# Attention adds moved to GpSimd by blocks, extra tiles at places 4 to 17, two tables made among the shared units, no closing GpSimd drain

## The reference, cut to what matters

```python
xn = layernorm(x)
# attention: each of 8 heads x 4 points picks one channel of the batch's first token
off = (xn @ W_off + b_off).reshape(B, N, 8, 4, 2)
w   = softmax((xn @ W_attn + b_attn).reshape(B, N, 8, 4), axis=-1)
idx = clip(wrap(int(off[..., 0])), 0, 127)
s   = sum(xn[:, 0, idx] * w)                     # one number per token
attn = broadcast(s, 128) @ W_out + b_out         # = s * colsum(W_out) + b_out
# feed-forward: 2 shared experts for all tokens, the best 2 of 8 routed ones per token
ffn(x, w1, w2, w3) = silu(x @ w1.T) * (x @ w3.T) @ w2.T
out = x + attn + sum(shared ffn) + sum(cw[e] * ffn_e(xn) for the 2 chosen e)
```

## Time and profile before

| | us |
|---|---|
| median of 3 runs | 418.75 (418.43 to 419.17) |
| span of the profiled execution | 416.8 |
| PE busy | 366.9 (88%) |
| DVE busy | 331.8 (80%) |
| ACT busy | 190.5 (46%) |
| POOL busy | 189.7 (46%) |

### The profile page before, as it was taken

One profiled execution on the slowest core, in us unless ns is written; L12 is line 12 of the kernel. 1 busy time (PEld: TensorE's weight loads), 2 busy tenths in 40 slices (PEclk: granted clock), 3 DMA queues, 4 the chain that ended last, 5 costly groups with the idle time before them and its releaser, 6 DMA issues.

```text
span 416.8 us, 12515 instructions
## 1 busy us (share of the span) xinstructions
PE 366.9 (88%) x4333; PEld 316.9 (76%) x4333; DVE 331.8 (80%) x929; ACT 190.5 (46%) x446; POOL 189.7 (46%) x152
## 2 busy tenths in 40 slices
PE   0157797789999999999999999999999999999990
PEld 0155564467677777777779999999999999999990
DVE  5988989987967699999996998886666666666760
ACT  2778728395322466666666344422222222222220
POOL 0434500404777776343200000001888888888863
PEclk9988999999999999999999999999999999999997
DMA  8944620000117199988873345554565956654332
GB/s 298 296 97 104 126 77 0 2 0 16 48 56 167 57 187 179 182 166 165 168 110 60 75 132 159 131 133 118 67 63 67 79 62 66 65 65 39 35 34 19
DMA packets 98871, 41.36 MB, mean 99 GB/s; under 512 B 73600, under 2 KB 92416, under 8 KB 98816
## 3 DMA queue, kind: packets, MB, share of 16 engines
q1 hardware_dynamic: 87120, 31.82, 36.7%
q0 software_dynamic: 11264, 8.69, 16.0%
q10 hardware_dynamic: 432, 0.11, 0.1%
HBM read 10.94 MB, written 12.88 MB: 57 GB/s over the span
## 4 chain that ended last, share of the span: by engine, by line
PE 74%; DVE 13%; ACT 6%; DMA 2%; issue 1%; POOL 1%; POOLq 0%; DVEq 0%; ACTq 0%
PE pY L832 18%; PE pY L655 11%; PE pAB L806 8%; PE pAB L804 8%; PE pAB L805 8%; PE pAB L643 5%; PE pAB L645 5%; PE pAB L644 5%; PE pV L667 4%; ACT units L870 3%; DVE hbuf L1189 2%; ACT wsp L941 2%; PE pV L621 2%; DVE hot L1095 1%; DMA xT<-hot 1%
## 5 line engine op out<-in xcount | busy, mean ns | idle before, releaser
L1065 POOL DMA_INDIRECT out_dram<-xT,rows x64 | 99.1, 1549 | 104.6 <-DMA out_dram<-base 83.3
L1011 ACT ACTIVATE units<-pAB 128x512 f32<-128x512 f32 x78 | 46.5, 596 | 119.6 <-PE pAB L806 119.6
L1053 POOL DMA_INDIRECT sorted_rows<-rows,slot x64 | 67.2, 1050 | 59.0 <-issue 32.3
L805 PE MATMUL pAB<-rows,wsp 128*128 128x128 f16 x512 | 89.0, 219 | 0.0
L806 PE MATMUL pAB<-rows,wsp 128*128 128x128 f16 x512 | 89.0, 219 | 0.0
L804 PE MATMUL pAB<-rows,wsp 128*128 128x128 f16 x512 | 89.0, 219 | 0.0
L832 PE MATMUL pY<-wsp,hbuf 128*128 (+1 forms) x620 | 86.4, 282 | 0.3 <-issue 0.3
L1476 DVE SCALAR_TENSOR_TENSOR hbuf<-pAB,units 128x512 f32<-128x512 f32 x78 | 53.6, 687 | 31.7 <-PE pAB L806 29.3
L832 PEld LDWEIGHTS pY<-wsp,hbuf 128*128 128x128 f32 x620 | 75.6, 192 | 0.8 <-issue 0.5
L655 PE MATMUL pY<-wsp,hbuf 128*128 128x128 f32 x512 | 70.2, 280 | 0.0
L655 PEld LDWEIGHTS pY<-wsp,hbuf 128*128 128x128 f32 x512 | 64.3, 192 | 4.1
(11 more groups left out here) (164 smaller groups left out, 586.1 us busy)
## 6 DMA issues: line engine op xcount, KB each, us to landing
base<-in_x SPq DMA_DIRECT2D x8, 512.0 KB, 7.5
out_dram<-base SPq DMA_DIRECT2D x16, 256.0 KB, 2.4
wraw<-in_wall SPq DMA_DIRECT2D x10, 256.0 KB, 2.8
rows<-hot SPq DMA_DIRECT2D x8, 256.0 KB, 2.7
proj<-sorted_rows SPq DMA_DIRECT2D x27, 68.5 KB, 1.9
wsp<-in_wall SPq DMA_DIRECT2D x10, 128.0 KB
sorted_rows<-rows,slot POOLq DMA_INDIRECT x64, 2.4
out_dram<-xT,rows POOLq DMA_INDIRECT x64, 3.4
```

What stands on the lines that cost most here:

```text
L805: pe.matmul(o, hi, x(1), start=False, stop=False)
L1053: pool.indirect_dma_start(sorted_rows, bass.IndirectOffsetOnAxis(ap=slot[:, t:t + 1].bitcast(U32), axis=0), rows[:, t, :], None, bounds_ch ...
L1065: pool.indirect_dma_start(out_rows, bass.IndirectOffsetOnAxis(ap=meta[:, t, DEST - CW:DEST - CW + 1].bitcast(U32), axis=0), yt[:, t], None ...
```

## The change

- **Extras at places 4 to 17.** `EXTRA_FROM` goes from 8 to 4. The list of jobs is otherwise the same.
- **Attention by blocks on GpSimd.** `r_attention` leaves VectorE's job loop (64 instructions of 128 elements). GpSimd gets `add_attention`: for each of the 16 blocks a product of `csum` and `attn_all` to a buffer of two (512 elements) and an addition to `base` (512 elements), the addition one block behind. It stands between the sorting scatters and the sends, and starts when `attn_saved` and `y_read` are complete.
- **Writes of blocks.** `WRITE_AT` now puts block i behind the loads of the turn eight after the one that ends with place i or later.
- **Tables.** `spread` is made before unit 22, straight behind the routing, in another buffer (`small`). TensorE's product and ScalarE's copy of it come with unit 25, and the copy lies in fp16 in a new buffer `sides16`, whose space `wp_raw` and `ident32` use before. `extra_table` follows before unit 24.
- **No GpSimd drain.** The `Block` is opened with `no_gpsimd_drain=True`.

```diff
-SPREAD_UNIT = UNITS - 4
+SPREAD_UNIT, SIDES_UNIT = 22, 25
...
-EXTRA_FROM = 8
+EXTRA_FROM = 4
...
-WRITE_AT = [min(n for n in range(AHEAD, STEPS) if FIRST_OF_TURN[n - AHEAD + 1] >= TPB * (i + 1) // ADDS + 5) for i in range(NB)]
+WRITE_AT = [min(n for n in range(AHEAD, STEPS) if LAST_OF_TURN[n - AHEAD] >= i) for i in range(NB)]
...
-        block = ctx.enter_context(nc.Block())
+        block = ctx.enter_context(nc.Block(no_gpsimd_drain=True))
...
+                if n == SIDES_UNIT:
+
+                    pe.wait_ge(table_ready, 1)
+                    pe.wait_ge(spread_ready, 1)
+                    for b in range(2):
+                        mm = pe.matmul(pV[:, b, :], c["ones"][:], spread.rearrange("p t m -> p (t m)")[:, b * BLK:(b + 1) * BLK],
+                                       start=True, stop=True)
+                    mm.then_inc(sides_done, 1)
...
-                if q == 1:
-                    spread_sides()
...
+                if n == SIDES_UNIT:
+                    act.wait_ge(sides_done, 1)
+                    nc.scalar.copy(sides16[:], pV[:].rearrange("p b c -> p (b c)")).then_inc(sides_ready, 1)
...
+            def add_attention():
+
+                for i in range(NB + 1):
+                    if i < NB:
+                        if i == 0:
+                            pool.wait_ge(attn_saved, APAIRS)
+                            pool.wait_ge(y_read, NB)
+                        if i >= 2:
+                            pool.wait_ge(attn_added, i - 1)
+                        nc.gpsimd.tensor_tensor(attn_part[:, i % 2], csum[:].unsqueeze(1).broadcast_to([P, TPB, P]),
+                                                attn_all[:, TPB * i:TPB * (i + 1)].unsqueeze(2).broadcast_to([P, TPB, P]),
+                                                ALU.mult).then_inc(attn_scaled, 1)
+                    if i:
+                        pool.wait_ge(attn_scaled, i)
+                        row = base[:, TPB * (i - 1):TPB * i, :]
+                        nc.gpsimd.tensor_tensor(row, row, attn_part[:, (i - 1) % 2], ALU.add).then_inc(attn_added, 1)
+
+            add_attention()
             pool.wait_ge(out_done, 16 * NB)
...
+            while unit[0] < SPREAD_UNIT:
+                shared_unit()
+            spread_out()
+            while unit[0] < ROUND * ATT - 8:
+                shared_unit()
+            extra_table()
...
-                if q == 1:
-                    extra_table()
...
-            def r_attention(g, r):
-                q = UNROLL * g + r
-                for tile in range(ADDS * q, min(ADDS * (q + 1), NT)):
-                    ins = add_attention(tile)
-                    if tile % TPB == TPB - 1:
-                        ins.then_inc(attn_added, 1)
```

More of the change, by code:

```diff
@@ L340, in layer_kernel @@
         yt = xT[:].rearrange("p i j s c -> p (i j s c)").bitcast(F32).rearrange("p (t c) -> p t c", c=P)
-        spread = hot_row[:, 0:TILES * 2 * E].rearrange("p (t m) -> p t m", m=2 * E)
-        sides = early[:, 512:1536].rearrange("p (t k e) -> p t k e", k=2, e=E)
+        spread = small[:].rearrange("p r c -> p (r c)").bitcast(F16).rearrange("p (t m) -> p t m", m=2 * E)
+        sides = sides16[:].rearrange("p (t k e) -> p t k e", k=2, e=E)
+        attn_part = aw_row[:, 0:2 * BLK].rearrange("p (r j c) -> p r j c", r=2, j=TPB)
         share_w = early[:, 1536:1664].rearrange("p (t k) -> p t k", k=2)
@@ L435, in layer_kernel @@
         attn_saved = sem("attn_saved")
+        attn_scaled = sem("attn_scaled")
         attn_added = sem("attn_added")
@@ L620, in routing_products @@
                     for a in range(NPAIR):
-                        mm = pe.matmul(pV[:, 1, 256:256 + NT], ident32[:], place[:, a, :], start=(a == 0), stop=(a == NPAIR - 1))
+                        mm = pe.matmul(pV[:, 1, 256:256 + NT], ident32, place[:, a, :], start=(a == 0), stop=(a == NPAIR - 1))
                     mm.then_inc(place_done, 1)
@@ L755, in _ @@
             straight(UNITS - ROUND, UNITS, both + [(0, first_addresses, UNITS - ROUND, UNITS)])
[L756 to L763, removed]
             def r_turn(g, r):
@@ L844, in _ @@
         def _(act):
-            for dst, src in [(wp_raw[:], wproj), (c["ident"][:], const["ident"]), (bp[:], bproj)]:
+            for dst, src in [(wp_raw, wproj), (c["ident"][:], const["ident"]), (bp[:], bproj)]:
                 act.dma_start(dst, src).then_inc(first_in, 16)
@@ L926, in exponentials @@
                 if n == ROWS_UNIT:
-                    nc.scalar.copy(ident32[:], c["ident"][:]).then_inc(ident_ready, 1)
+                    nc.scalar.copy(ident32, c["ident"][:]).then_inc(ident_ready, 1)
                     for r in range(4):
@@ L1412, in routed_low @@
                     split_low(g - (ATT - 1), u // 4)
[L1415 to L1422, removed]
             def extra_table():
@@ L1434, in extra_table, with spread_out @@
                 v.scalar_tensor_tensor(active[:], f(0), 0.0, f(1), ALU.is_gt, ALU.mult).then_inc(extras_ready, 1)
[L1436 to L1443, removed]
+            def spread_out():
+                dve.wait_ge(table_done, 1)
+                v.tensor_tensor(spread, c["ident"][:, 0:TILES].unsqueeze(2).broadcast_to([P, TILES, 2 * E]),
+                                tab_f[:, 2:2 + 2 * E].unsqueeze(1).broadcast_to([P, TILES, 2 * E]),
+                                ALU.mult).then_inc(spread_ready, 1)
+            while unit[0] < SPREAD_UNIT:
[4 more added lines that the diff above has]
+            extra_table()
+            assert unit[0] == ROUND * ATT - 8
+            for n in range(8):
+                shared_unit()
+                one_hot(ATT - 1 + (n + 4) // ROUND, (n + 4) % ROUND)
+                if n >= 6:
+                    weighted_high(ATT - 1, n)
             start, end = ROUND * ATT, UNITS
@@ L1450, in _ @@
             rounds(dve, ATT + 1, UNITS // ROUND - 1, both)
-            straight(UNITS - ROUND, UNITS + 4, both + [(0, spread_out, UNITS - ROUND, UNITS)])
+            straight(UNITS - ROUND, UNITS + 4, both)
             extra_tile = {}
@@ L1546, in y_second @@
                                            ).then_inc(d_y, 1)
[L1548 to L1561 removed]
             pipeline(dve, NJOB, UNROLL, NJOB // UNROLL, [(4, side_sums), (4, y_first), (4, y_second), (2, r_hf), (3, side_products),
[L1563 removed]
+                                                         (4, load_tiles), (2, extra_shares)])
 def kernel(**inputs):
```

20 lines of the change are left out of this document (7 added, 13 removed).

## The result

The changed kernel takes **414.02 us** (median of 4 runs, 413.80 to 414.45) against 418.90 of the kernel before (4 runs): ratio 0.9886, 95% interval 0.9872 to 0.9900. The forecast was 414.1. The profiled execution took 413.85 us with a span of 411.9; before it was a span of 416.8, so 4.9 us have gone from inside the span. Around it lie 1.95 us in this execution, as the forecast took for the kernel before; over the four runs it is 1.75 to 2.2.

What follows compares the result with a forecast made beforehand. TensorE was taken to bound the kernel until 405.7 us, then GpSimd's sends and drain: 416.8 - 4.3 - 0.4 + 0 = 412.1 for the span, with 1.95 around it 414.1 us; range 413.0 to 418.6.

Steps and rivals of the forecast that it cites:

- The bound: From about 100 to 405.7 us TensorE's matmuls run without a gap, one step of the extras every 2.51 us.
- The drain, -4.3: At the closing barrier the core waits only for GpSimd's drain, 412.2 to 416.5; leaving it out saves 4.3 us.
- Rival 2: The drain comes back outside the span, so only the tail is gained and runs show 418.3; chance 0.15.
- The tail of sends, -0.4: GpSimd's last sends: without backlog the last goes up to 0.83 us earlier, nothing if the gap returns; taken -0.4.
- The attention adds, 0: 32 GpSimd instructions of 1.14 us, 38 us from 225, last block at 263; VectorE gets 0.78 us free; 0 us.
- VectorE beside GpSimd: In the extras only two shares (0.14 us) can be locked out; waiting once, VectorE's step is 2.30, under 2.51.
- Rival 1: VectorE becomes the bound as GpSimd takes turns between its two shares; chance 0.12 in full, 0.08 mild.
- mild form: VectorE's first share hardly waits, the second waits for GpSimd: 2.7 us longer, 416.8 us; chance 0.08.
- full one: VectorE's step becomes 3.44 us in 11 steps beside GpSimd: +8.2 us, time 422.3; chance 0.12.
- Rival 3: GpSimd's adds take over 2 us each, so the first send passes 291.8; at 2.4 us, 427; chance 0.03.
- SyncE's queue: Loads of rows behind block writes that wait for GpSimd still land in time, 2 us to spare; 0 us.
- tables: Table work among the shared units makes two VectorE products some 0.3 us late; 0 us, bounds -0.4 and +0.5.

Runs made afterwards that it cites:

- experiment 2: The kernel before with only GpSimd's closing drain left out (no_gpsimd_drain=True): 414.55 us, ratio 0.9910.
- experiment 6: The changed kernel with the attention adds back on VectorE, three a step, and the block writes where they stood before: 414.14 us.
- experiment 1: The changed kernel with GpSimd's closing drain put back: 418.69 us against 418.68 before, ratio 1.0001.
- experiments 1 and 3: The one numbered 3: the changed kernel with the extras at places 8 to 21 again, as before the change: 414.43 us.
- experiment 12: The changed kernel with GpSimd's drain back and only the first 48 of the 64 sends: 408.99 us (one run).
- experiment 5: The changed kernel with 40 idle products on GpSimd before the first send: 430.15 us.
- experiment 11: The changed kernel with GpSimd's drain back and only the last 16 of the 64 sends: 418.77 us, ratio 0.9998.

## Why the prediction was right

- **The bound.** Right: TensorE without a gap, steps of 2.51, last second products at 403.48 (403.72 before).
- **The drain, -4.3.** Right, by itself (-4.1 in the runs with that edit alone) and by its removal from the change (+4.7, 414.02 to 418.69). Rival 2, that it comes back outside the span, is refuted for the drain as a whole: with GpSimd's drain all runs on record have 1.9 to 2.1 us around the span, without it 1.7 to 2.5. So a few tenths of the 4.3 may come back in some runs, most evenly in experiment 2 (2.2 to 2.3 in all four).
- **The tail of sends, -0.4.** The profile shows these 0.40 (408.53 to 408.13), but not for the reason given, and most of it is not the change's. That step took the first free send to go 0.2 us behind its y (405.64 to 405.85). In the trace it is 0.89: y of the last tile but one ends at 405.39, its send starts at 406.28. Applied to the kernel before this gives 405.64 + 0.89 + 1.85 = 408.38 for the last send, 0.15 before its 408.53, and not 0.83. The measured difference between the two orders is 0.16 (408.29 in experiment 2 to 408.13). The other 0.24 is there without the change too: the last second products start 0.23 earlier in experiment 2 than in the execution profiled first. The large gap came back at the same place, and of it the prediction had said that nothing is then gained; but it came back as 1.60 us instead of 1.96, and the next send but one then waits for y. The term should have been -0.15, and that the range held is no proof of its reason: experiment 6 has the first send as late as before and the same -0.15. What the 0.15 hangs on is this shorter gap, whose cause stays open.
- **The attention adds, 0.** Right, by experiments 1 and 6. The estimate of 1.14 us an instruction was one number for two: 1.04 for the product, 1.27 for the addition, mean 1.16; the last block at 262.6 where 263 was forecast. That the first send goes at 271.96 where 271 was forecast is in part luck: the prediction had the last block in DRAM by 265.4 (263 and 2.4) and y as the gate, but in this execution the gate was the write that SyncE issued only at 267.34. In experiment 1, where the gate was y, the first send goes at 270.19.
- **VectorE beside GpSimd.** Right in what decides: the pair of shares waits once, for no more than one instruction (0.22 to 0.89 us together in nine steps of eleven beside GpSimd, 1.07 and 1.31 in the two others), and the step stays at 2.51. Beside GpSimd hbuf keeps its 0.69 us and the additions to yt their 0.34, while an instruction of another line with two inputs in SBUF (`side_products`, L1508) took 0.84 us at 227.71 and 0.18 at 404.15, without GpSimd's adds. By the Trainium skill, "SBUF — State Buffer", section "Who interferes with whom", an instruction of VectorE with two inputs in SBUF is locked out by a GpSimd instruction that reads SBUF, and one with at most one input there, outside the 2-port modes, is not. The trace agrees.
- **Rival 1** did not occur. Its mechanism is real, and the runs with shares apart show it: GpSimd gets a turn between two of them. Its price does not hold for the case it was set for. Two shares apart cost 1.4 to 1.5 us in the medians and at most 2.6 (416.64), up to the price of the mild form (416.8), not the 8.2 of the full one. That three shares apart came to 3.57 us a step and 421.7 us, near the 3.44 and 422.3 of the full form, is luck: the price counted eleven steps over all 38 us of GpSimd's work, but the first shares come at 235.93, 11 us after its first add, so at 3.44 us a step only eight fit, and 8 x 0.93 - 2.0 is 5.4. The 2.0 us that VectorE may be late do fit: with three shares the eight steps from 234.63 to 263.66 are 8.95 us longer than eight of 2.51, and TensorE's last second products start 7.23 later. What kept the rival away is the reason that was put against it: shares that follow each other at once leave GpSimd no turn. One wait between them is enough to lose up to 2.6 us.
- **Rival 3**: refuted, the longest of the 32 instructions took 1285 ns. Its threshold of 291.8 comes out at 291.3, and the one run behind it lost as much as its first send was late.
- **SyncE's queue, extras from place 4, tables: 0 each.** In sum this holds (experiments 1 and 3). VectorE's products were later than forecast, though: the one behind the spread product starts at 116.72, 0.7 us after ScalarE had its input ready (115.99), and the next at 119.38, 1.2 after (118.18), where 0.3 was forecast. TensorE waits for neither, and VectorE idles 1.14 us again at 123.01. TensorE's matmuls for the table only moved: in the chain of waits its first second products start at 227.26 instead of 227.11 (experiment 2) and its last at 403.48 instead of 403.49.

No variant here that writes the whole output is faster than the changed kernel by more than the runs can tell; the kernel before with the drain left out has all but at most 0.5 us of its gain.

## What to carry to other kernels

When a change has several parts, ask first which of them lies behind the last instruction of the engine that bounds the kernel: here one flag was all of it, and the other parts moved work between engines that had room. Look at the closing block's rows for an engine whose drain ends after everything that the output needs; if it issued its last work more than its drain's length before the end, as in experiment 12, the drain is free, otherwise it is on the path. And when work moves to an engine for whose instructions another stands back, count how many *separate* small instructions of the other meet it in a step, not how long they are: each can wait for one whole instruction, so three small instructions that take 0.54 us together without GpSimd made a step of 3.57 us out of one of 2.51.

## What the runs showed that was not expected

- GpSimd's drain took 9.13 to 9.41 us behind 16, 48 or 64 sends alike, also with nothing left to wait for that the trace shows.
- The turns cost one side alone: with four shares a step in its way, GpSimd's additions took 1.26 to 1.28 us as without, while each of VectorE's shares, under 0.2 us when nothing holds it, took up to 1.2. That GpSimd loses nothing because a share is so short is not shown.
- A send that is not waited behind another starts 0.89 us after the y that it waits for (405.39 to 406.28), and 0.30 behind the send before it when it has a backlog. So a chain of waits of GpSimd's sends has two prices, and the one in a full queue hides the other.
- A gap of 1.60 to 1.96 us without a releaser stands before the 61st send in every variant that makes all 64 sends and has free ones at the end. It is gone with a full queue (experiment 5), and also where only the last 16 are made (experiment 11), so it does not belong to that tile. What it is was not found.
